# A mixture-of-experts layer on one core: the adapter stage's first quantising pass put between squares and evacuation, and a common scale computed two stages earlier

## The reference, cut to what matters

```python
x = x + L0_ffn(L0_cond(x, itok_B_0_3))       # x: (8, 512, 256), 4096 rows
x = x + L1_ffn(L1_cond(x, itok_B_0_8))

def L0_cond(x, ids):                         # low-rank map, one of 4 per sequence
    return (x @ A[ids].T) @ B[ids].T + emb[ids]
def quant(x, clip):                          # one scale for the whole tensor
    scale = sigmoid(clip) * max(abs(x)) / 127
    return clip(round(x / scale), -128, 127) * scale
def L0_ffn(x):                               # weights are quantised row by row
    xq = quant(x, clip_x)
    h = quant(silu(xq @ wg.T) * (xq @ wu.T), clip_down)
    return h @ wd.T
def L1_cond(x, ids):                         # adapter, one of 10 per sequence
    h = relu(x @ W1[ids] + b1[ids])
    y = x + h @ W2[ids] + b2[ids]
    return (y - mean(y)) / sqrt(var(y) + 1e-5) * gamma[ids] + beta[ids]
def L1_ffn(x):                               # 9 experts, the 2 best per row
    p, idx = top_k(softmax(x @ Wr), 2);  p = p / sum(p)
    return sum over the 2 of p * ((silu(x @ Wg[idx]) * (x @ Wu[idx])) @ Wd[idx])
```

## Time and profile before

| | |
|---|---|
| three runs | 761.05 us median, 752.59 to 768.59 |
| profiled execution | 762.39 us, span 760.7 us, mean granted TensorE clock 0.904 |
| busy | PE 637.3 us (84%), DVE 524.3 (69%), ACT 445.4 (59%), POOL 375.7 (49%) |
| chain of waits, by engine | PE 61%, ACT 10%, issue 9%, DVE 8%, DMA 5%, SPq 4% |
| stage 1 and what lies between | 0 to 72 us |
| stage 2 | 72 to 141 us |
| stage 3 | 141 to about 292 us |
| stage 4 | from about 292 us, PE busy 434.6 of 468.7 us |

### The profile page before, as it was taken

The page is one execution under the profiler, slowest core; times in us unless marked ns, Lnnn a source line. Parts: engine busy times, 40 slices in busy tenths (PEclk is TensorE's granted clock), DMA queues, the critical chain, the costliest instruction groups (busy, mean ns, idle before and its releaser), DMA issues.

```text
span 760.7 us, 15623 instructions
## 1 busy us (share of the span) xinstructions
PE 637.3 (84%) x4165; PEld 399.8 (53%) x4165; DVE 524.3 (69%) x1356; ACT 445.4 (59%) x739; POOL 375.7 (49%) x586
## 2 busy tenths in 40 slices
PE   5797868487687725599999999999999999999982
PEld 1213323254454413366666767777666777777761
DVE  5413899546777767788878888888777566666551
ACT  2324878257777654467777777677666445544540
POOL 2100444100666657545556666666665555555533
PEclk9755999579989965789999999999999999999997
DMA  6421100022455493867789979897577577656652
GB/s 194 129 70 37 54 1 0 2 84 77 147 171 161 137 324 119 232 115 147 169 169 182 194 154 171 180 155 157 100 140 140 100 114 100 119 100 112 105 82 41
DMA packets 160436, 94.80 MB, mean 125 GB/s; under 512 B 112980, under 2 KB 153572, under 8 KB 160356
## 3 DMA queue, kind: packets, MB, share of 16 engines
q1 hardware_dynamic: 146660, 75.28, 43.4%
q0 software_dynamic: 13696, 18.51, 14.0%
HBM read 44.20 MB, written 23.61 MB: 89 GB/s over the span
## 4 chain that ended last, share of the span: by engine, by line
PE 61%; ACT 10%; issue 9%; DVE 8%; DMA 5%; SPq 4%; POOL 2%; POOLq 0%; DVEq 0%; ACTq 0%
PE ps L1100 28%; PE ps L1148 17%; DMA out<-small 3%; PE ps L770 3%; PE ps L750 3%; ACT big L710 3%; PE ps L673 3%; PE ps L519 2%; PE ps L448 2%; PE ps L1078 2%; ACT small L801 2%; ACT big L389 1%; ACT small L677 1%; DMA small<-in_xT 1%; POOL rows L897 1%
## 5 line engine op out<-in xcount | busy, mean ns | idle before, releaser
L1100 PE MATMUL ps<-big,small 128*128 x1608 | 252.0, 313 | 0.7 <-ACT small L1113 0.7
L1100 PEld LDWEIGHTS ps<-big,small 128*128 128x128 f16 x1608 | 151.8, 98 | 84.8 <-issue 1.3
L1170 POOL DMA_INDIRECT out<-small x67 | 110.7, 1652 | 158.4 <-DVE small L1166 145.9
L1148 PE MATMUL ps<-big,small 128*128 (+1 forms) x1139 | 142.7, 273 | 5.9 <-DVE small L1166 3.3
L1148 PEld LDWEIGHTS ps<-big,small 128*128 128x128 f16 (+1 forms) x1139 | 107.9, 97 | 32.4 <-issue 20.9
L1122 ACT ACTIVATE small<-small 128x704 f16<-128x704 f32 x67 | 52.8, 789 | 89.9 <-DVE small L1119 89.5
L1119 DVE SCALAR_TENSOR_TENSOR small<-ps,small 128x704 f32<-128x704 f32 x67 | 63.6, 950 | 37.0 <-PE ps L1100 35.8
L1136 DVE SCALAR_TENSOR_TENSOR small<-small 128x64 f16<-128x64 f32 (+1 forms) x134 | 72.4, 582 | 20.3 <-ACT small L1130 20.1
L1155 POOL TENSOR_SCALAR small<-small 128x1 f32<-128x1 f32 x67 | 80.4, 1200 | 0.0
L1130 ACT ACTIVATE small<-small 128x704 f16<-128x704 f32 x67 | 59.1, 882 | 29.6 <-DVE small L376 29.6
L897 POOL DMA_INDIRECT rows<-small x64 | 65.6, 1025 | 18.0 <-issue 16.4
(11 more groups left out here) (208 smaller groups left out, 1037.2 us busy)
## 6 DMA issues: line engine op xcount, KB each, us to landing
small<-rows SPq DMA_DIRECT2D x67, 130.0 KB, 2.7
big<-in_Wg SPq DMA_DIRECT2D x8, 704.0 KB, 5.0
big<-in_Wu SPq DMA_DIRECT2D x8, 704.0 KB, 6.3
big<-in_Wd SPq DMA_DIRECT2D x8, 640.0 KB, 5.3
small<-in_xT SPq DMA_DIRECT2D x8, 512.0 KB, 4.0
small<-in_xT SPq DMA_DIRECT2D x16, 256.0 KB, 3.1
out<-big SPq DMA_DIRECT2D x16, 256.0 KB, 2.8
rows<-small SPq DMA_DIRECT2D x10, 130.0 KB, 2.4
```

The costliest lines, as they stand in the source:

```text
L1100: m = put("pe", ("gate", "up")[j], [tk["xsT", t], free, *start, *converted(t, j)], lambda e, h=h, k=k, xp=xp, wp=wp, n=n: e.matmul(ps[:, 2 ...
L1148: tk["dn", t] = put("pe", "dn", [tk["hT", t], mk("yw", t - 1), *converted(t, 2)], lambda e, n=n, w=w, hc_=hc_, wp=wp, c=c: e.matmul(ps[:, ...
L1170: tk["add", t] = dma("pool", f"add{t % 2}", [tk["yw", t], *stored, *(tk["pads"] if t >= SOLO else [mk("add", t - 2)])], lambda e: e.indire ...
```

## The change

It has two parts. In `cond`, `st_hy` (the first pass, for the piece that will be used in two steps) is called behind `st_squares` instead of behind `adapter_gate`; what stood in it for the second pass is now `st_hu`, and stays where it was. The computation of the common scale is taken from ahead of step 0 and spread: the two loads stand behind the clip factors in SP's queue, the first three operations behind `centre`, with the matmul on TensorE, and the rest behind `quant_x(0)`. TensorE's first products of stage 2 wait for the last of them (`kxun`), since the small matmul's result lies in a PSUM bank that they write. The buffer `gb` moves to a place that stages 1 and 2 don't use.

```diff
--- before.py
+++ after.py
@@ -195,7 +195,6 @@
         pk = carve(small, a, [8])
         OH = carve(small, a, [2, 36], BF16)
         posI = [carve(small, a, [2, 4], I32) for _ in range(4)]
-        gb = carve(small, a, [2, 32])
         cmp9, hot9 = [carve(small, a, [E, E]) for _ in range(2)]
         a[0] = max(a[0], stages_end)
         xk = carve(small, a, [2, 512])
@@ -203,6 +202,7 @@
         bWr = carve(small, a, [NB * E])
         W2G = carve(small, a, [NB * EC])
         eps2 = carve(small, a, [2])
+        gb = carve(small, a, [2, 32])
         assert a[0] <= 14000, a
 
         al = [32768]
@@ -470,6 +470,10 @@
         lcl = dma("sp", "clip", [], lambda e: e.dma_start(cl[:, 1:2], clips[1].partition_broadcast(P)))
 
 
+        kgb = None
+        for r, v in enumerate((gam, bet)):
+            kgb = dma("sp", "gb", [], lambda e, r=r, v=v: e.dma_start(gb[0:80, r, :], v.rearrange("a (u n) -> (a u) n", n=32)))
+
         def quant_w(j, st, n, qb, landed, free):
 
             m = put("dve", "wq", [landed, kedge], lambda e: e.tensor_reduce(swg[:, j, 0:n], st, AX, ALU.max,
@@ -603,6 +607,10 @@
 
 
         kg = centre(kcol)
+        m = put("dve", "xb", [kgb], lambda e: e.tensor_reduce(xsc[0:80, 0:2], gb[0:80], AX, ALU.max, apply_absolute_value=True))
+        m = put("dve", "xb", [m], lambda e: e.scalar_tensor_tensor(xsc[0:80, 2:3], xsc[0:80, 0:1], 16.0, xsc[0:80, 1:2], ALU.mult, ALU.max))
+        m = put("dve", "xb", [m, kx], lambda e: e.tensor_scalar(spread[0:80, 0:80], ident[0:80, 0:80], xsc[0:80, 2:3], None, ALU.mult))
+        kxb = put("pe", "xbp", [m, *first_done, ev], lambda e: e.matmul(ps[:, 6, 256:336], onesf[0:80, :], spread[0:80, 0:80], start=True, stop=True))
 
         S = 16
         tk = {}
@@ -661,12 +669,21 @@
                                                                      ALU.max))
 
         quant_x(0)
+        m = put("dve", "xb", [kxb], lambda e: e.tensor_reduce(xsc[:, 6:7], ps[:, 6, 256:336], AX, ALU.max))
+        m = put("dve", "xb", [m], lambda e: e.tensor_scalar(xsc[:, 4:5].bitcast(I32), xsc[:, 6:7].bitcast(I32), EXPO, None, ALU.bitwise_and))
+        m = put("dve", "xb", [m], lambda e: e.tensor_scalar(xsc[:, 4:5], xsc[:, 4:5], 2.0 ** -60, 2.0 ** -13, ALU.max, ALU.mult))
+        m3 = put("dve", "xb", [m], lambda e: e.reciprocal(xsc[:, 3:4], xsc[:, 4:5]))
+        kbws = put("dve", "xb", [kg, m3], lambda e: e.tensor_scalar(bWr, bWr, xsc[:, 3:4], None, ALU.mult))
+        m = put("dve", "xb", [m], lambda e: e.tensor_tensor(xsc[:, 5:6], xsc[:, 4:5], xsc[:, 4:5], ALU.mult))
+        put("dve", "xb", [m], lambda e: e.tensor_scalar(eps2[:, 0:1], xsc[:, 5:6], 1.0 / H, None, ALU.mult))
+        kxun = put("dve", "xb", [m], lambda e: e.tensor_scalar(eps2[:, 1:2], xsc[:, 5:6], 1e-5, None, ALU.mult))
+        tk["xun"] = kxun
 
         n = 0
         for b in range(NB):
             for c in range(6):
                 w, s = P, n % 4
-                first = [kz, cdone[NB - 1], ev, tdone[NB - 1], xqd[b], kg]
+                first = [kz, cdone[NB - 1], ev, tdone[NB - 1], xqd[b], kg, kxun]
                 for j, wT in enumerate((wgT, wuT)):
                     for k in range(2):
                         m = put("pe", "gu", [*first, (sil if j == 0 else freeu).get(n - 4)],
@@ -708,6 +725,9 @@
         def st_hy(s):
             v = hB[:, s // 2, :, 256 * (s % 2):256 * (s % 2) + 256]
             tk["hy", s] = put("act", "hy", [kh], lambda e: e.activation(v, v, ACT.Copy, bias=MAGIC, scale=sc[:, 3:4]))
+
+        def st_hu(s):
+            v = hB[:, s // 2, :, 256 * (s % 2):256 * (s % 2) + 256]
             if s >= EARLY:
                 tk["hu", s] = put("act", "hy", [tk["hy", s], mk("pd", s - 2), kneg, *l0], lambda e: e.activation(
                     hq[:, s % 2], v, ACT.Relu, bias=negm))
@@ -900,22 +920,6 @@
 
         scattered = []
 
-        kgb = None
-        for r, v in enumerate((gam, bet)):
-            kgb = dma("sp", "gb", l0, lambda e, r=r, v=v: e.dma_start(gb[0:80, r, :], v.rearrange("a (u n) -> (a u) n", n=32)))
-        m = put("dve", "xb", [kgb], lambda e: e.tensor_reduce(xsc[0:80, 0:2], gb[0:80], AX, ALU.max, apply_absolute_value=True))
-        m = put("dve", "xb", [m], lambda e: e.scalar_tensor_tensor(xsc[0:80, 2:3], xsc[0:80, 0:1], 16.0, xsc[0:80, 1:2], ALU.mult, ALU.max))
-        m = put("dve", "xb", [m], lambda e: e.tensor_scalar(spread[0:80, 0:80], ident[0:80, 0:80], xsc[0:80, 2:3], None, ALU.mult))
-        m = put("pe", "xbp", [m, *l0], lambda e: e.matmul(ps[:, 6, 0:80], onesf[0:80, :], spread[0:80, 0:80], start=True, stop=True))
-        m = put("dve", "xb", [m], lambda e: e.tensor_reduce(xsc[:, 6:7], ps[:, 6, 0:80], AX, ALU.max))
-        m = put("dve", "xb", [m], lambda e: e.tensor_scalar(xsc[:, 4:5].bitcast(I32), xsc[:, 6:7].bitcast(I32), EXPO, None, ALU.bitwise_and))
-        m = put("dve", "xb", [m], lambda e: e.tensor_scalar(xsc[:, 4:5], xsc[:, 4:5], 2.0 ** -60, 2.0 ** -13, ALU.max, ALU.mult))
-        m3 = put("dve", "xb", [m], lambda e: e.reciprocal(xsc[:, 3:4], xsc[:, 4:5]))
-        kbws = put("dve", "xb", [kg, m3], lambda e: e.tensor_scalar(bWr, bWr, xsc[:, 3:4], None, ALU.mult))
-        m = put("dve", "xb", [m], lambda e: e.tensor_tensor(xsc[:, 5:6], xsc[:, 4:5], xsc[:, 4:5], ALU.mult))
-        put("dve", "xb", [m], lambda e: e.tensor_scalar(eps2[:, 0:1], xsc[:, 5:6], 1.0 / H, None, ALU.mult))
-        tk["xun"] = put("dve", "xb", [m], lambda e: e.tensor_scalar(eps2[:, 1:2], xsc[:, 5:6], 1e-5, None, ALU.mult))
-
         def bc9(v, inner):
             return v.rearrange("p (a n) -> p a n", a=1).to_broadcast([P, E, E]) if inner else v.rearrange(
                 "p (n a) -> p n a", a=1).to_broadcast([P, E, E])
@@ -945,6 +949,7 @@
 
             rb, odd = divmod(i - 5, 2)
             at(4, st_squares)
+            at(0, st_hy)
             at(2, st_x1T)
             at(1, st_hq)
             at(4, st_var)
@@ -962,7 +967,7 @@
             at(2, st_ad)
             if i % 2 == 1 and i < 2 * NB:
                 adapter_gate(i // 2)
-            at(0, st_hy)
+            at(0, st_hu)
             at(3, st_ln)
             at(4, st_logit)
             at(4, st_aff)
```

## The result

The changed kernel takes **727.75 us** (median of 4 executions, 725.45 to 728.49) against 762.5 for the kernel before (median of the 4 beside it, 752.59 to 768.59): ratio 0.961, 95% interval 0.951 to 0.971. I had forecast 744 with a range of 737 to 752. In two later batches, on two different chips, the same program gave 728.53 (ratio 0.966, 0.961 to 0.972) and 739.35 (0.972, 0.966 to 0.979). So the gain is sure and its size is not one number; why it is not takes up a large part of what follows.

The account below looks back on a forecast made before the run. ScalarE was taken to own the adapter loop's period. Terms -4.9 + 0.9 + 2.2 - 1.6 - 4.8 - 9.0 = -17.2 gave 745.2 from the profiled 762.4, 743.9 from the median, so 744 us; range 737 to 752.

Parts of the forecast that it names:

- Steps 7 to 17: Pipelined adapter steps in stage 3: 66.6 us instead of 75.6, -9.0, with bounds -5 and -10.4.
- VectorE's loop in odd steps, GpSimd's in even ones: Bounds of adapter steps 7 to 16 after the change: 6.57 us odd, 6.33 even, a pair 12.9.
- the 1.4 for such spells: Steps 7 to 17: 1.4 us added for TensorE products at half clock, two such odd steps of five remaining.
- TensorE stays at the high clock: Rival: shorter idle time removes slow products in steps 4 to 17, 4.6 us more gain, 739 to 740; chance 0.20.
- Steps 4 to 7: Adapter stage: the moved first pass leaves the path in three steps, 3 x 1.6 = -4.8 us.
- the scale at the start of stage 3: Without the scale chain, the first quantising operation starts at 142.6 instead of 147.5 us: -4.9.
- SP's two issues: Stage 1: two loads issued ahead of a block of x on SP's queue, 0.47 us each: +0.9.
- the operations between the stages: Between stages 1 and 2: VectorE's three and eight scale operations delay the first matmul of stage 2: +2.2 us.
- The whole to step 4: From stage 3's first pass to step 4's power operation: -6.5 us, from the scale (-4.9) and step 2's moved pass (-1.6).
- GpSimd falls behind: Rival, slower: scatters in steps 7 to 17 lengthen beside busier VectorE; decides from some 2.0 us between scatters; chance 0.04.
- The estimate of some 165 us: Rule against the change: VectorE's port lock could stretch a scatter to 4.8 us, 44 adding some 165, about 910 total.
- Partly given back: Rival: slow spells remain, the front costs more, or the tail keeps its date: -8 to -13, 748 to 753; chance 0.24.

Follow-up runs that it names:

- e14: The kernel before, unchanged, run again beside the changed kernel: 762.04 us (ratio 1.002).
- e1: The kernel before, unchanged, run again with a trace: 758.08 us (ratio 1.002).
- e2: The kernel before with only the first pass moved, the common scale staying ahead of step 0: 747.49 us beside 758.83 (ratio 0.981).
- e4: The kernel before with two unused loads of gamma and beta added where the change has them: 759.42 us (ratio 1.002).
- e5: The changed kernel, unchanged, run again: 728.53 us (ratio 0.966).
- e13: The changed kernel, unchanged, run again on another chip: 739.35 us (ratio 0.972).
- e6: The changed kernel with twenty extra bf16 matmuls in TensorE's two idle times of stage 1, results unread: 725.59 us.
- e7: The kernel before with the same twenty extra bf16 matmuls in TensorE's idle times of stage 1: 748.38 us.
- e11: The changed kernel with the payload's row numbers written by ScalarE instead of GpSimd's iota: 741.92 us (ratio 0.978).
- e8: The changed kernel with the common scale computed inside stage 1, at turns 5 and 6: 729.93 us (ratio 0.967).
- the fourth batch: Changed kernel (739.35 us), kernel before (762.04), and two repeated edits of the changed kernel (738.47 and 741.91), with the kernel before beside them at 759.20.
- third and fourth batch: Third: four edits of the changed kernel, 738.40 to 741.92 us; fourth: changed kernel unchanged, kernel before and two of those edits again, changed kernel 739.35.
- the first batch: The kernel before unchanged, with two unused loads, with only the pass moved, and with only the scale moved: 758.08, 759.42, 747.49 and 755.73 us.

## Why the prediction was off

**The step that failed is the base.** The sum was laid "Against the profiled execution of 762.4 (span 760.7)", and everything outside the change was put at nothing. One stretch outside it is not fixed: 36 matmuls at the end of stage 1, whose time follows the clock that they get. In the traces without extra matmuls they take 17.9, 19.5 and 32.4 us in the kernel before (e14, e1, and the shown one, to which e2 and e4 are alike) and 18.3, 22.7 and 19.5 in the changed one (the shown one, e5, e13). The profile that I used had the slowest case, and its own timeline said so, 21.5 us apart (TensorE, kernel before):

```profile
17.72 1.89 PE L448 MATMUL ps<-small 128*16 128x512 f32 x4
...
39.26 3.60 PE L448 MATMUL ps<-small 128*16 128x512 f32 x4
```

14.1 of the 17.2 us between the forecast -17.2 and the -34.4 of the two spans are this row. The scatter of the three executions, 752.6 to 768.6, was the sign: I read it as noise of the measurement, but 16 us is about the size of this stretch at half clock. My range of 15 us had no case for it. With the clock held in both kernels the change is worth -22.8 (e6 and e7), 5.6 more than forecast; that part is the next two paragraphs.

**Steps 7 to 17 were mis-sized: -12.0 instead of -9.0.** The form was right (VectorE's loop in odd steps, GpSimd's in even ones, which e11 bears out for the odd ones), but both lengths were too long. The even step takes 5.95, not 6.33: the iota takes 0.16 there, not the 0.38 that I took from the earlier trace rows, and the power operation starts before the iota has ended, where I had added a hand-over. The iota takes 0.38 where it falls beside VectorE's line 743 (189.69 in 189.30 to 190.03), and the new order moves that meeting into the odd step, where GpSimd waits anyway. The odd step takes 6.39, not 6.57, mainly since line 743 now starts 0.79 behind line 756 instead of 0.93. One step of 6.65 is the only one with a slow spell, so the 1.4 for such spells was mostly not needed either: that part of the rival "TensorE stays at the high clock" came true. The granted clock of the shown pair is 0.98 instead of 0.88.

**Steps 4 to 7** gave -5.0 for -4.8, which is luck: step 6 was slow in this execution (8.13). In e5, e6, e8 and e13 the three steps take 19.4 to 19.8, where the traces of before have 25.7 to 27.9; between e6 and e7 it is -6.4. The rival had both slow spells of TensorE vanish here. One does: step 4's products take 1.18 instead of 1.63. Step 6's stay slow in part (2.18 in the shown execution and in e6, 1.41 in e5).

**Right:** the scale at the start of stage 3 (-4.8 for -4.9), SP's two issues (+0.9 for +0.9), the operations between the stages (+2.4 for +2.2, +2.1 between e6 and e7), and nothing behind step 17 (+0.1). The whole to step 4 (-6.9 for -6.5) is right in this pair of executions; between e6 and e7 it is -4.9, where the kernel before had waited 1.21 us for its load of beta instead of 2.68. Stage 2's +1.4 is no effect of the change that repeats: it takes 68.3 to 70.3 us in the traces of the changed kernel and 68.7 to 69.7 in those of before, and +0.2 between e6 and e7.

**The rivals.** "GpSimd falls behind" is refuted in its size: a scatter takes 0.999 us on the mean at 88% VectorE load against 1.002 at 76%, and the scatters stay 1.28 us apart. What there is of interference is the 0.2 us of the iota. Its premise was right: GpSimd is now a link of the bound. The estimate of some 165 us from the Trainium skill (SBUF — State Buffer; its 620 and 3100 ns stand in the section "A bandwidth-pool intuition that's wrong (but worth ruling out)") is not borne out by any of the traces. "Partly given back" said -8 to -13 and came true nowhere: even in the fourth batch, where the changed kernel takes 739.35, it lies 19.9 below the kernel before. "TensorE stays at the high clock" with its 4.6 more gives -21.8, close to the -22.8 of e6 and e7; that is in part luck, since the start of stage 3 gave less there than forecast and steps 7 to 17 gave more.

**What is open.** It is not shown why the clock of stage 1 rises early, late or not at all; the runs show only that the time of the rise differs between executions of either program, and that work ahead of the run prevents the low case. Nor is it shown whether the changed program meets the low case less often. What makes the releases late in the third and fourth batch is open too: slower landings of some weights go with them, but the first batch has such landings and hardly any stall, and no run separated a chip, its neighbours or the delivery of instructions.

## What to carry to other kernels

Before a sum is laid on one profiled execution, compare equal shapes within it: a stretch whose matmuls take twice what the same ones take elsewhere may run at the other clock in the next execution, and then it belongs in the range with both its lengths. If executions of one program scatter by more than a per cent, look for such a stretch first; filling TensorE's idle time ahead of it cost twenty matmuls here and gave the kernel before 6.5 us and a scatter of 6 instead of 14. A loop whose bounding engine has hardly any idle time left (0.24 us in 12.34) should be measured on more than one chip: the changed kernel took 728.5 us on one and 739.4 on another.

## What was not expected of the hardware

- TensorE busy 32.41 of 32.50 us at a granted clock of 0.50 throughout, with matmuls of 16 output rows or 16 contraction rows in fp32. Continuous work alone didn't raise it. The same run was at 0.91 in another execution.
- 3.2 us of idle time in such a run (e8) were followed by a group of 3.60 us instead of 1.89.
- The same program on different chips: 728.5 and 739.35 us, with landings of 640 KB after 5.4 and 8.1 us, while the kernel before differs by 4 (754.9 and 759.2). The program with the moved pass alone (e2) had slow landings on a third chip and took 65.4 us in steps 7 to 17, 1.8 more than the changed kernel on the fast one.
- GpSimd's iota of 128x2 takes 0.37 to 0.47 us where it overlaps VectorE's quantising operation (line 743, 1536 columns in bf16) and 0.12 to 0.16 otherwise, also beside other operations of VectorE. That holds for every iota of stage 3 in seven traces looked through (before, after, e2, e5, e6, e7, e13). The scatters beside the same operation take 0.96 to 1.11 us in these traces; of the others most take the same.

The best version that ran is e6, the changed kernel with the twenty extra matmuls: 725.59 us against 728.53 beside it.
